# Features and scores from raw x, center sums on TensorE, inverse norms on VectorE

## The reference

```python
x = x + conv_ref(_ln_c(x), Wf, bf, Wv, bv, Wp, bp, sim_alpha, sim_beta)   # _ln_c: (x - mean) / sqrt(var + 1e-6), over channels
# conv_ref, for each quarter image and head:
f = Wf @ x + bf;  v = Wv @ x + bv
cen = mean of f over 4 x 4 blocks of 7 x 7 tokens;  vc = the same of v
cen_n = cen / max(|cen|, 1e-12);  tok_n = f / max(|f|, 1e-12)
sim = sigmoid(sim_beta + sim_alpha * cen_n . tok_n);  sim = sim * onehot(argmax over centers)
agg = (sim @ v + vc) / (sim.sum + 1);  out = Wp @ (sim^T @ agg) + bp
# then t = t + ffn(_ln_t(t)): two layers with sign weights and a quantization over a group of images
```

## Time and profile before

| | |
|---|---|
| median of 3 runs | 3021.69 us (3013.63 to 3026.43) |
| profiled execution, span from first to last instruction | 3014.8 us |
| what the median has beyond that span | 6.9 us |
| busy: PE, DVE, ACT, POOL | 2860.9, 2683.4, 2177.4, 2014.7 us |
| a plain slot, from one `eq` to the next | 18.27 us |

### The profile page before, as it was taken

One profiled execution on the slowest core, in us unless ns is written; L12 is line 12 of the kernel. 1 busy time (PEld: TensorE's weight loads), 2 busy tenths in 40 slices (PEclk: granted clock), 3 DMA queues, 4 the chain that ended last, 5 costly groups with the idle time before them and its releaser, 6 DMA issues.

```text
span 3014.8 us, 62753 instructions
## 1 busy us (share of the span) xinstructions
PE 2860.9 (95%) x20998; PEld 1934.8 (64%) x20998; DVE 2683.4 (89%) x5540; ACT 2177.4 (72%) x4510; POOL 2014.7 (67%) x4275
## 2 busy tenths in 40 slices
PE   3999999999999999999999999999999999999987
PEld 2666666556666665666666566666665666666554
DVE  3788888999999989999999999999999999998975
ACT  1677777897767779777777886777789777777952
POOL 1566666677777768777777347777767777776354
PEclk9999999999999999999999999999999999999997
DMA  1011111002222210122222012222200222221034
GB/s 45 17 40 34 33 33 33 9 17 65 66 65 65 65 49 1 49 65 65 66 73 65 10 33 70 74 68 65 57 25 17 65 65 65 66 65 49 1 94 132
DMA packets 30932, 154.29 MB, mean 51 GB/s; under 512 B 6483, under 2 KB 6804, under 8 KB 30612
## 3 DMA queue, kind: packets, MB, share of 16 engines
q1 hardware_dynamic: 30612, 150.28, 17.8%
HBM read 75.60 MB, written 74.66 MB: 50 GB/s over the span
## 4 chain that ended last, share of the span: by engine, by line
POOL 58%; issue 21%; PE 13%; DVE 4%; ACT 3%; POOLq 1%; SPq 0%; DMA 0%; DVEq 0%; ACTq 0%
POOL eq L442 7%; POOL mo_x L384 6%; POOL mo_t L384 6%; PE ps L1102 4%; PE ps L1046 4%; POOL turns L468 4%; POOL tok L452 3%; POOL mo_x L379 3%; ACT turns L579 2%; POOL cinv L436 2%; POOL n2c L399 2%; DVE turns L844 2%; POOL csq L394 2%; PE ps L969 1%; POOL nxy L411 1%
## 5 line engine op out<-in xcount | busy, mean ns | idle before, releaser
L969 PE MATMUL ps<-wfT,xn 97*112 97x384 f32 x1792 | 735.9, 518 | 0.3 <-ACT sq L523 0.2
L1046 PE MATMUL ps<-tok,w1T 98*128 98x392 f16 x2880 | 599.7, 330 | 13.5 <-ACT turns L582 8.7
L523 ACT ACTIVATE sq<-ps 112x384 f32<-112x384 f32 x896 | 431.0, 489 | 207.8 <-PE ps L969 204.8
L468 POOL CAST turns<-turns 128x392 f16<-128x392 f32 x240 | 324.9, 1367 | 206.1 <-ACT turns L579 201.9
L1046 PEld LDWEIGHTS ps<-tok,w1T 98*128 98x128 f16 x2880 | 269.5, 97 | 226.1 <-issue 61.1
L707 DVE TENSOR_REDUCE n<-sq 112x32 f32<-112x1536 f32 (+1 forms) x256 | 396.0, 1547 | 20.9 <-ACT sq L523 6.8
L774 DVE TENSOR_REDUCE hmax<-ps 128x1 f32<-128x392 f32 x720 | 382.1, 558 | 33.7 <-PE ps L1046 28.1
L969 PEld LDWEIGHTS ps<-wfT,xn 97*112 97x112 f32 x1792 | 271.7, 180 | 213.9 <-DVE cosb L717 65.5
L529 ACT ACTIVATE sig<-cosb,betac 112x896 f32<-112x896 f32 x128 | 133.3, 1041 | 312.2 <-DVE cosb L717 312.2
L492 ACT ACTIVATE xnT<-ps,mo_x 112x96 f32<-112x96 f32 x896 | 304.4, 454 | 62.2 <-POOL mo_x L386 62.2
L579 ACT ACTIVATE turns<-ps,scale 128x1176 f32<-128x1176 f32 x240 | 323.0, 1346 | 36.1 <-DVE scale L797 34.5
(11 more groups left out here) (143 smaller groups left out, 6125.8 us busy)
## 6 DMA issues: line engine op xcount, KB each, us to landing
xbuf<-in_x SPq DMA_DIRECT2D x64, 588.0 KB, 4.6
out<-xbuf SPq DMA_DIRECT2D x64, 588.0 KB, 6.0
turns<-out SPq DMA_DIRECT2D x60, 588.0 KB, 6.3
out<-turns SPq DMA_DIRECT2D x60, 588.0 KB, 4.4
tok<-in_L_ffn_W SPq DMA_DIRECT2D x2, 142.5 KB
cst<-in_constants SPq DMA_DIRECT2D x1, 195.0 KB
wf<-in_L_conv_Wf SPq DMA_DIRECT2D x1, 144.0 KB
tok<-in_L_conv_Wv SPq DMA_DIRECT2D x1, 144.0 KB
```

The costliest lines, as they stand in the source:

```text
L468: nc.gpsimd.tensor_copy(ghi[:, k % 3, HT:2 * HT], gel[:, k % 3, HT:2 * HT]).then_inc(b_mid, 1)
L523: nc.scalar.activation(sq[:, t, :], bank(2 + t % 2, TN, D), ACT.Square).then_inc(f_sq, 1)
L969: mm(bank(2 + t % 2, TN, D), xn[:, k % 2, t * TN:(t + 1) * TN], wfT[:, :], start=True, stop=True)\
L1046: ins = mm(dst, w1T[:, c * 128:(c + 1) * 128], tok[:, bass.ds(place, 1), part, s * HT:(s + 1) * HT].rearrange("p a n -> p (a n)"), start=p ...
```

## The change

1. `features` and `scores` no longer read the normalised `xn` but the raw quarter `xq`. The mean goes by taking the mean over channels off each row of Wf once at the start. The inverse deviation is not applied: the cosine does not depend on a token's scale. So that the bias has the same scale, the row under the 96 channels holds the token's deviation instead of ones. POOL computes it (`x_std`), PE transposes the seven columns (`std_back`), ACT copies them to `stdT` and issues **seven DMAs** that put them into the row of `xq` (`row_of_std`). `xq` has three buffers. The floor of a token's squared norm is multiplied by its variance.
2. `x_back` and `copy_x` go. The centers' sums are made on PE from `xnT`: seven matmuls with a 0/1 matrix of 32 columns, four of them side by side in the array (`token_sums`), a copy on ACT, one matmul that adds the four parts (`center_sums`), a copy of 16 columns on DVE in place of `pooled`'s reduction.
3. The inverse norms move from POOL to DVE: a guess and one step with a product of two quadratics, nine instructions instead of twelve.
4. `q_scaled`, `q_placed` and `shares` move from DVE to ACT; alpha goes into the sigmoid's scale.
5. All engines' lists are written in a new order.

```diff
-        xn = sb("xn", [C + 1, 2, QN])
+        xq = sb("xq", [C + 1, XQ, QN])
+        stdT = sb("stdT", [T, 2, TN])
+        csum = sb("csum", [HM, C + 1])
...
                     done(pool, s + "_rstd", q)
+                    if s == "x":
+                        nc.gpsimd.tensor_tensor(w[:, 10, :], w[:, 7, :], w[:, 8, :], ALU.mult).then_inc(S["x_std"], 1)
                     nc.gpsimd.tensor_tensor(w[:, 9, :], w[:, 3, :], w[:, 8, :], ALU.mult).then_inc(S[s + "_shift"], 1)
...
-            def copy_x(part):
...
+            def copy_std(k, q, place, use):
+                done(act, "std_T", q)
+                nc.scalar.copy(stdT[:, k % 2, :], bank(0, T, TN)).then_inc(S["std_copied"], 1)
+
+            def row_of_std(k, q, place, use):
+                done(act, "std_copied", q)
+                for t in range(T):
+                    act.dma_start(xq[C:C + 1, q % XQ, t * TN:(t + 1) * TN], stdT[t:t + 1, k % 2, :]).then_inc(row_in[q % XQ], 16)
+
+            def copy_sums(k, q, place, use):
+                done(act, "sum_ps", q)
+                done(act, "cen_ps", q - 1)
+                nc.scalar.copy(csum[:, :], bank(0, HM, C + 1, 384)).then_inc(S["sum_copied"], 1)
...
             def attention(part):
-                return [(R, 1, normalise("t", 6, 1), FFN), (A, 1, copy_sim(0)), (R, 1, n_high(0, part), FFN),
...
+                return [(X, 1, copy_sums), (A, 0, sigmoid), (X, 0, gather), (M, 0, squares(0, 4)), (X, 1, q_scaled),
...
+            step(v.reduce_sum(wfsum[:, :], wf[:, :, 0:C], AX.X))
+            step(v.tensor_scalar(wfmean[:, :], wfsum[:, :], 1.0 / C, None, ALU.mult))
+            step(v.tensor_tensor(wf[:, :, 0:C], wf[:, :, 0:C], wfmean[:, :].unsqueeze(2).broadcast_to([C, 4, C]), ALU.subtract))
...
             def pooled(k, q, place, use):
 
-                done(dve, "xn_copied", q)
+                done(dve, "cen_ps", q)
                 done(dve, "u_done", q - 4)
-                blocks = xn[:, k % 2, :].rearrange("c (a r b w) -> c a b r w", a=4, r=PW, b=4)
-                v.tensor_reduce(cenx[:, k % 4, :].rearrange("c (a b) -> c a b", a=4), blocks, AX.XY, ALU.add)\
-                    .then_inc(S["cen_x"], 1)
+                v.tensor_copy(cenx[:, k % 4, :], bank(0, C + 1, CENTERS, 488)).then_inc(S["cen_x"], 1)
...
+            def norm_part(k, q, place, use):
+                done(dve, "n_guess", q)
+                v.tensor_tensor(ny2[:, :], ninv[:, :], ninv[:, :], ALU.mult).then_inc(S["n_square"], 1)
+                done(dve, "n_square", q)
+                v.tensor_tensor(nh[:, :], ny2[:, :], n2c[:, :], ALU.mult).then_inc(S["n_part"], 1)
...
+            def token_sums(k, q, place, use):
+                done(pe, "x_norm", q)
+                done(pe, "std_copied", q)
+                blocks = const("blocks", TN)
+                for t in range(T):
+                    c = t % TA * 32
+                    ins = mm(ps[c:c + 32, 0, 384:384 + C + 1], blocks[:, t * 32:(t + 1) * 32], xnT[:, k % 4, t, :],
+                             start=t < TA, stop=t + TA >= T)
+                ins.then_inc(S["sum_ps"], 1)
+
+            def center_sums(k, q, place, use):
+                done(pe, "sum_copied", q)
+                mm(bank(0, C + 1, CENTERS, 488), csum[:, :], const("gathered"), start=True, stop=True).then_inc(S["cen_ps"], 1)
...
                     for t in range(t0, t1):
-                        if t in (0, TA):
-                            done(pe, "xn_copied0" if t == 0 else "xn_copied", q)
+                        if t == 0:
+                            pe.wait_ge(row_in[q % XQ], (q // XQ + 1) * (16 * T))
                         if t >= 2:
                             reached(pe, f_sq, q * T + t - 1)
-                        mm(bank(2 + t % 2, TN, D), xn[:, k % 2, t * TN:(t + 1) * TN], wfT[:, :], start=True, stop=True)\
+                        mm(bank(2 + t % 2, TN, D), xq[:, q % XQ, t * TN:(t + 1) * TN], wfT[:, :], start=True, stop=True)\
                             .then_inc(f_ps, 1)
```

More of the change, by code:

```diff
@@ L24 @@
 XB = 4
+XQ = 3
 BODY = 2 * XB
@@ L49, in shape_constants @@
     parts["bias_part"] = np.stack([p == C, p == C + 1], 1)
+    t, m = np.arange(T), np.arange(32)
+    token = t[None, :, None] * TN + p[:, None, None]
+    block = token // QS // PW * 4 + token % QS // PW
+    parts["blocks"] = np.where((block == m) & (p[:, None, None] < TN), 1.0, 0.0).reshape(128, T * 32)
+    parts["gathered"] = p[:, None] % 32 == np.arange(CENTERS)
     parts["last_row"] = np.stack([p == C, p == C], 1)
@@ L171, in build @@
         S = {n: sem("s_" + n) for n in NAMES}
+        row_in = [sem(f"row_in{j}") for j in range(XQ)]
         f_ps, f_sq = sem("f_ps"), sem("f_sq")
@@ L524, in squares, with q_scaled, q_placed, shares @@
                 return step
+            def q_scaled(k, q, place, use):
+                done(act, "cen_inv", q)
+                nc.scalar.activation(qT[:, :], bank(0, HM, C + 1, 128), ACT.Copy, scale=cinv[:, k % 2:k % 2 + 1])\
+                    .then_inc(S["q_scaled"], 1)
+            def q_placed(k, q, place, use):
+                done(act, "q_T", q)
+                done(act, "s_ps", q - 2)
+                nc.scalar.copy(Q[:, k % 2, :], bank(0, C + 1, HM, 256)).then_inc(S["q_done"], 1)
+            def shares(k, q, place, use):
+                done(act, "a_rden", q)
+                done(act, "o_ps", q - 1)
+                nc.scalar.activation(aggp[:, :], bank(5, HM, C), ACT.Copy, scale=rden[:, :]).then_inc(S["a_done"], 1)
             def sigmoid(k, q, place, use):
@@ L528, in sigmoid @@
                 done(act, "sim_done", q - 2)
-                nc.scalar.activation(sig[:, k % 2, :], cosb[:, :], ACT.Sigmoid, bias=betac[:, :]).then_inc(S["sig_done"], 1)
+                nc.scalar.activation(sig[:, k % 2, :], cosb[:, :], ACT.Sigmoid, bias=betac[:, :], scale=alphac[0:TN, :]).then_inc(S["sig_done"], 1)
             def copy_eq(k, q, place, use):
@@ L741, in denominators @@
                 v.reciprocal(rden[:, :], bank(5, HM, 1, C)).then_inc(S["a_rden"], 1)
-            def shares(k, q, place, use):
-                done(dve, "a_rden", q)
-                done(dve, "o_ps", q - 1)
-                v.tensor_scalar(aggp[:, :], bank(5, HM, C), rden[:, :], None, ALU.mult).then_inc(S["a_done"], 1)
             def residual(half):
@@ L819, in attention @@
             def attention(g, part):
-                return [(M, 1, norms(TA, T)), (R, 1, n_low(0), FFN), (R, 1, n_low(1), FFN), (A, 1, summed),
-                         (R, 1, h_largest(0, 2), FFN), (A, 1, denominators), (A, 1, shares),
-                         (R, 1, h_largest(2, 3), FFN), (R, 1, h_largest(3, 4), FFN),
-                         (X, 1, pooled), (R, 1, h_largest(4, 5), FFN), (M, 1, cosine), (X, 1, centers), (A, 1, residual(0)),
-                         (R, 1, h_largest(5, 6), FFN), (A, 1, residual(1)), (X, 1, center_floor),
-                         (A, 0, maxima), (X, 1, q_scaled), (R, 0, stats("t", 6, g), FFN),
-                         (X, 1, q_placed), (M, 0, norms(0, TA)),
-                         (X, 0, stats("x", 0)), (A, 0, masked), (R, 0, finish(part), FINAL)]
+                return [(M, 1, norm_guess), (M, 1, norm_part), (M, 1, norm_factors), (R, 1, n_low(0), FFN),
+                        (M, 1, norm_inverse), (R, 1, n_low(1), FFN), (R, 1, h_largest(0, 1), FFN), (A, 1, summed),
+                        (R, 1, h_largest(1, 3), FFN), (A, 1, denominators), (M, 1, cosine),
+                        (R, 1, h_largest(3, 5), FFN), (X, 1, pooled), (A, 1, residual(0)), (A, 0, maxima),
+                        (X, 1, centers), (R, 1, h_largest(5, 6), FFN), (A, 1, residual(1)), (X, 1, center_floor),
+                        (R, 0, stats("t", 6, g), FFN), (R, 0, finish(part), FINAL), (M, 0, norms(0, TA)),
+                        (X, 0, stats("x", 0)), (A, 0, masked), (M, 0, norms(TA, T))]
             def group(g, part):
@@ L908, in to_tokens, with std_back @@
                 return step
-            def x_back(part):
-                t0, t1, _, _, end = BANKS[part]
-                def step(k, q, place, use):
-                    done(pe, "x_norm" + end, q)
-                    for t in range(t0, t1):
-                        ins = tr(bank(part, C + 1, TN, (t - t0) * TN), xnT[:, k % 4, t, :], ident[0:TN, 0:TN])
-                    ins.then_inc(S["xn_ps" + end], 1)
-                return step
+            def std_back(k, q, place, use):
+                done(pe, "x_std", q)
+                done(pe, "x_norm0", q)
+                tr(bank(0, T, TN), mo["x"][:, k % 2, 10, :], ident[0:TN, 0:TN]).then_inc(S["std_T"], 1)
+            def token_sums(k, q, place, use):
[10 more added lines that the diff above has]
+                mm(bank(0, C + 1, CENTERS, 488), csum[:, :], const("gathered"), start=True, stop=True).then_inc(S["cen_ps"], 1)
             def centers(k, q, place, use):
                 done(pe, "cen_x", q)
-                done(pe, "xn_copied", q)
                 for c in range(4):
```

129 lines of the change are left out of this document (55 added, 74 removed).

## The result

| | before | after |
|---|---|---|
| median of the runs | 3023.37 us (3013.63 to 3026.43, 4 runs) | 4122.29 us (4118.91 to 4132.05, 4 runs) |
| ratio | | 1.366 (95%: 1.363 to 1.369) |
| span of the profiled execution | 3014.8 us | 4130.3 us |
| mean granted TensorE clock | 0.988 | 0.798 |
| a plain slot, `eq` to `eq` | 18.27 us | 27.2 us in the median |

What follows compares the result with a forecast made beforehand. The bound was a closed loop through four engines, 18.27 us a slot, with no single engine full. 24 x 0.63 + 92 x 0.88 = 96 us on 3014.8, less 5, plus 6.9, gave about 3110 us, range 2960 to 3220.

Steps and rivals of the forecast that it cites:

- The loop and its order: The new slot's chain through the engines in group 0, from the start of `pooled`: VectorE ready at 18.1 us, ACT's branch 18.9.
- TensorE's own work: Transposes go and narrow matmuls come on TensorE: costed at 0, between -0.5 and +0.3 us a slot.
- GpSimd's relief alone: GpSimd loses the 12 inverse-norm instructions, which have no place in the loop: costed at nothing.
- ACT's seven issues: Seven DMA issues per slot on ACT, ahead of `copy_sums`: 0.29 us each, 2.03 us in which ACT starts nothing else.
- the row that is alike: A one-partition DMA row on SP, 0.25 us long with the next 0.29 behind it, taken as price of an ACT issue.
- the fork: Behind the reciprocal at 16.2 us: VectorE's branch ready at 18.1, ACT's issues, `copy_sums` and `center_sums` at 18.9; the later counts.
- VectorE stands idle 0.8 us ahead of `pooled`: At the slot's end VectorE waits 0.8 us for ACT's branch, making the slot 18.9 us, 0.63 more than before.
- `finish` term: In 92 plain slots of groups 1 to 4, VectorE's `finish` holds GpSimd's t moments: 0.25 us a slot, 0 to 0.5.
- The first rival: ACT's issues cost little and hide beside VectorE's work: 23 to 93 us off, 2930 to 3000 us; chance 0.25.
- The 50 ns: The Trainium skill's figure for the sequencer's dispatch of a DMA, cited for issues being cheap on ACT.
- The second rival: TensorE's `features` wait for the last row, landing in 3 to 4 us: 3190 to 3300 us; chance 0.12.
- The signs: What the changed kernel's trace should show: `eq` 18.9 to 19.3 us apart, ACT's issues 0.25 to 0.3 apart, `cenx` idle 0.7 to 1.0.

Runs made afterwards that it cites:

- e1: The kernel after with its seven row DMAs of a slot put into one issue on ACT; 1.014 of before.
- e3: The kernel after, seven issues kept, with seven unread matmuls on TensorE just ahead of `center_sums`; 3484.83 us, 1.158 of before.
- e8: The kernel after with four row DMAs per slot in place of seven, two rows each and the last one row; 1.062 of before.
- e10: The kernel after with one row DMA per slot, `clipped` waiting for VectorE's last norm operation, and `finish` doing 8 of its 784 columns; 0.991 of before.
- e7: The kernel after with one row DMA per slot and GpSimd's `clipped` waiting for VectorE's last norm operation of the slot; 1.012 of before.
- e2: The kernel after without the row DMAs and TensorE's wait for them, the row set to ones once; 3035.1 us, 1.008 of before.

## Why the prediction was wrong

- **The loop and its order: right, nearly to the tenth.** In e1, group 0, from `cenx` (297.22): the norm chain starts at 308.64, 11.4 behind (said: 11.4); the second `n_low` ends at 311.50, 14.3 (14.2); the reciprocal ends at 313.24, 16.0 (16.2); VectorE is at the next `cenx` at 315.30, 18.1 (18.1). TensorE's own work: 2837.9 us in e1, 2860.9 before, -0.2 a slot (-0.5 to +0.3). The nine norm operations: 0.18 to 0.22 each, 1.45 to the first `n_low` (1.4). That GpSimd's relief alone is worth nothing was not tested.
- **ACT's seven issues: the mechanism right, the size wrong.** The step reads "I take 0.29, by the row that is alike", between "zero, and 0.42 a piece". It was 0.50 for the first and 0.64 from one to the next, 4.35 us instead of 2.03, and outside both bounds. The row was alike in its one partition and unlike in its source (HBM, not SBUF). And it was the cheaper of two equal loads: the other, 0.50 in the same trace, lay above the upper bound already. With 4.35 in place of 2.03 the fork gives 16.2 + 4.35 + 0.7 = 21.2; e3 measured 21.49. This is some 270 us of the miss.
- **TensorE's clock: a term that was missing.** "VectorE stands idle 0.8 us ahead of `pooled`", and TensorE with it; the sum then took every duration behind that at the rows of a kernel whose clock was 0.988. At 0.8 us that would have held (e8: 0.9 us idle, clock 0.987). At 3 us it cost 643 us, the largest part of the miss. The wrong size and the missing term go together: the low price hid that the wait would be long enough to matter for the clock. Of the 1012 us of the miss some 100 are in neither of the two; the `finish` term below is about 33 of them, the rest is open.
- **The `finish` term: half seen.** 0.25 was taken, "0 to 0.5" the bounds. The collision of the t moments with `finish` alone is worth 0.52 (e10 to e7), at the upper bound; with that of `nh` with `clipped`, which was not foreseen, it is 0.61 (e10 to e1).
- **The first rival (the issues fit beside VectorE's work)**: its mechanism is e1's, but its time was too low. Even with no row at all (e2) the kernel takes 3035 us, 1.008 of before, and not 2930 to 3000, for those two collisions; e10, without them, takes 0.991 of before. The 50 ns that stood for it are not the price of an issue here, and "less to describe than any on SP" did not make it cheap.
- **The second rival (the row arrives late)**: not so. The landing of 1.7 us lies in the 1.5 to 2.5 estimated, and no feature waits for it in the kernel after (in e1, 8.0 us in all).
- **The signs**: seven rows on ACT's queue ahead of `csum`, `cenx` waiting for `center_sums`, TensorE waiting for `csum`, norm operations of 0.2 us, one t moment of 0.8 us or more: all seen. 0.25 to 0.3 apart, 0.7 to 1.0 us idle ahead of `cenx` (3.35) and 18.9 to 19.3 a slot: not. Beside the 0.42 a piece, a slow transfer was the only thing named that could make it slower still; none of the signs was TensorE's clock.
